# Grouped attention on one Trainium2 core: SP issues Q's loads between Q's stores and K's stores

## The reference, cut to what matters

```
q = (h @ Wq).reshape(b, s, H, HD)            # H = 16 heads, HD = 8
k = (h @ Wk).reshape(b, s, HKV, HD)          # HKV = 4 heads
v = (h @ Wv).reshape(b, s, HKV, HD)
q = _apply_rope(q, cos, sin)
k = _apply_rope(k, cos, sin)
...
scores = jnp.einsum('bqhd,bkhd->bhqk', q, k) / np.sqrt(HD).astype(np.float32)
scores = jnp.where(causal[None, None], scores, jnp.finfo(scores.dtype).min)
attn = jax.nn.softmax(scores, axis=-1)
ctx = jnp.einsum('bhqk,bkhd->bqhd', attn, v).reshape(b, s, H * HD)
```

## Time and profile before

| | us |
|---|---|
| median of 3 runs | 3165.83 |
| lowest, highest | 3156.24, 3166.15 |
| the profiled execution's own time | 3165.76 |
| its span, first to last instruction | 3164.0 |
| around the span (3165.76 - 3164.0) | 1.76 |
| grouped attention, about | 520 to 1260 |

### The profile page before, as it was taken

How to read it: one execution, slowest core, us unless ns; L and a number is a source line. 1 busy time by engine, 2 the same in 40 slices (tenths; PEclk the granted TensorE clock), 3 DMA queues, 4 the chain that set the end, 5 groups by cost and what they waited for, 6 DMA issues and landing times. The chain is left out here.

```text
span 3164.0 us, 66212 instructions
## 1 busy us (share of the span) xinstructions
PE 2882.8 (91%) x22258; PEld 1871.3 (59%) x22258; DVE 2482.6 (78%) x6944; ACT 2326.2 (74%) x3601; POOL 2104.2 (67%) x2402
## 2 busy tenths in 40 slices
PE   6999997788998888789579999999999999999979
PEld 3555554344444444678246666666666666666668
DVE  5777776788888875567468888888888888888867
ACT  5888883466666667444289999999999999999833
POOL 5666673346555543577657888788877888788745
PEclk8999997799999999899789999999999999999989
DMA  4544534223322330685400000000000000000001
GB/s 121 131 108 112 129 92 91 59 62 69 69 57 60 72 70 19 191 271 158 128 1 1 17 1 17 1 7 11 6 12 1 17 1 17 1 17 1 1 14 41
DMA packets 151509, 178.31 MB, mean 56 GB/s; under 512 B 18619, under 2 KB 122784, under 8 KB 151076
## 3 DMA queue, kind: packets, MB, share of 16 engines
q1 hardware_dynamic: 142084, 157.14, 19.2%
q0 software_dynamic: 9088, 16.94, 1.6%
HBM read 99.82 MB, written 75.95 MB: 56 GB/s over the span
## 5 line engine op out<-in xcount | busy, mean ns | idle before, releaser
L3380 PE MATMUL lb_FF<-lb_h,lb_w 128*128 128x512 f32 x1024 | 502.0, 592 | 0.0
L3609 DVE TENSOR_SCALAR lb_z<-lb_M,lb_mv,lb_rstd 128x128 f32<-128x128 f32 x1024 | 344.9, 398 | 3.3 <-POOL lb_rstd L3534 3.0
L3497 ACT ACTIVATE lb_h<-lb_H,lb_prm 128x512 f32<-128x512 f32 x512 | 327.5, 699 | 2.6 <-PE lb_H L3371 2.6
L3534 POOL TENSOR_TENSOR lb_rstd<-lb_rstd,half 128x4 f32<-128x4 f32 x256 | 260.8, 1019 | 37.2 <-issue 1.3
L3365 PE MATMUL lb_H<-lb_x1s,lb_w 128*128 128x512 f32 x512 | 273.0, 533 | 0.0
L3380 PEld LDWEIGHTS lb_FF<-lb_h,lb_w 128*128 128x128 f32 x1024 | 193.5, 189 | 89.9 <-issue 61.1
L3601 DVE BATCH_NORM_STATS2 lb_stats<-lb_M 128x6 f32<-128x128 f32 x1024 | 226.9, 284 | 15.5 <-PE lb_M L3324 9.0
L1649 POOL TENSOR_SCALAR_AFFINE_SELECT da_PT<-da_PT 128x1024 f32<-128x1024 f32 x128 | 149.1, 1165 | 133.4 <-ACT da_PT L1566 133.3
L3366 PE MATMUL lb_H<-lb_x1s,lb_w 128*128 128x512 f32 x512 | 203.3, 397 | 0.0
L3371 PE MATMUL lb_H<-lb_x1s,lb_w 128*128 128x512 f32 x512 | 202.7, 397 | 0.1
L3552 POOL CAST lb_x1s<-lb_x 128x512 fp32r<-128x512 f32 x128 | 78.3, 611 | 173.7 <-DVE lb_x L3634 173.7
(11 more groups left out here) (514 smaller groups left out, 8860.8 us busy)
## 6 DMA issues: line engine op xcount, KB each, us to landing
moe_w<-experts_dram SPq DMA_DIRECT2D x39, 384.0 KB, 3.2
da_qT<-da_stq SPq DMA_DIRECT2D x64, 192.0 KB, 4.1
da_kT<-da_stk SPq DMA_DIRECT2D x64, 192.0 KB, 3.8
moe_x<-moe_xs SPq DMA_DIRECT2D x39, 260.0 KB, 3.6
tc_g<-moe_ys SPq DMA_DIRECT2D x32, 256.0 KB, 3.5
ga_q<-ga_stq SPq DMA_DIRECT2D x20, 384.0 KB, 5.8
lb_split<-moe_parts SPq DMA_DIRECT2D x8, 896.0 KB, 6.4
da_stq<-da_parts SPq DMA_DIRECT2D x16, 384.0 KB, 2.4
```

Source lines behind the costliest of these rows:

```text
L3380: pe.matmul(FF[:, :], w2[:, k, :], h[:, k, :], start=(k == 0), stop=(k == KC - 1)).then_inc(ff_filled, 1)
L3497: act.activation(h[:, k, :], H[:, k % 2, :], ACT.Gelu_apprx_tanh, bias=col(FB1 + k, i)).then_inc(h_ready, 1)
L3534: pool.tensor_tensor(out[:, :], out[:, :], C["half"][:, 0:NT], ALU.pow).then_inc(done, 1)
L3609: last = v.tensor_scalar(z[:, t, :], M[:, t * P:(t + 1) * P], mv[:, t, 0:1], rstd[:, t:t + 1], ALU.subtract, ALU.mult)
```

## The change

SP issues `load_q(c2)` directly behind `store_q(c2)`, ahead of `store_k(c2)`. Before, both groups of stores came first. No instruction is added or removed, on no engine, and no semaphore count changes.

```
@@ -1065,8 +1065,8 @@
                 c, c2 = b + 1, b + 2
                 if exists(c2):
                     store_q(c2)
+                    load_q(c2)
                     store_k(c2)
-                    load_q(c2)
                     load_k(c2)
                 if exists(c):
                     store_max(c)
```

## The result

The changed kernel takes 3174.18 us (median of 7 runs, 3171.63 to 3180.1), the kernel before in the same comparison 3162.6 us (7 runs, 3156.24 to 3166.15). The ratio is 1.0043, with a 95% interval of 1.0031 to 1.0054: slower, by 11.6 us between the medians.

The account below looks back on a forecast made before the run. The prediction took PE's restart in each batch to be set by the landing of K's second load. It added 19 us of later landings and 7 us of lower clock to 3165.76, giving 3192 us, range 3170 to 3210.

Parts of the forecast that it names:

- The place and the mechanism: PE's restart once a batch follows K's second load, which the change delays by putting K's stores behind Q's loads.
- the chain after: From landing of Q's third store to landing of K's second load in the changed kernel: 12.4 us, against 11.0 before.
- SP's reactions: SP's delay after Q's third store lands and again after K's stores land, 0.05 us each.
- Q's loads, issue to second landing: From issue of Q's first load to landing of its second: 7.4 us, bounds 6.9 to 7.8.
- K's stores behind them: Time K's stores still need after Q's second load lands: 0.7 us, bounds 0.3 to 1.0.
- K's loads in an empty queue: K's two loads, issued only after K's stores land, from issue to last landing: 4.2 us, bounds 3.95 to 4.5.
- the 2 us absorbed: PE's later waits for DVE, in batches 11, 8 and a little in 5 and 13, hide about 2 us of 21.
- the clock: Longer PE stops send 5 further restarts to the lower clock level, 1.45 us each, 7 us.
- The late third stores: In batches 1, 4, 5, 12, 13 Q's loads now wait for Q's late third store: K lands 2.7 us later.
- Rival 1: K's stores are not held up by Q's loads, so K lands 1.5 us earlier: 3147 us, chance 0.08.
- Rival 2: The delay is absorbed by DVE after restarts, or the terms' cheap ends hold: 3170 us, chance 0.12.
- Rival 3: The terms' expensive ends, 13.4 us, with ten clock losses: 3216 us, chance 0.05 for beyond 3210.

Follow-up runs that it names:

- q_half: Kernel before, with K's stores issued between Q's two loads and K's loads last: 3150.8 us, ratio 0.9965 to the kernel before.
- the pair with the masks: after_mask8 against before_mask8, the mask repeated eight times in both: 0.9991 against 0.9963, slower by 0.28% or 9 us.
- wait_only: Kernel before, plus a wait of SP for the landing of Q's stores ahead of K's stores, loads not moved: ratio 1.0023 to the kernel before.
- before_again: The kernel before, unaltered, profiled a second time: 612.9 us from first to last of the 15 batches.
- after_again: The changed kernel, unaltered, profiled a second time: 3185.36 us in this single execution, 630.4 us from first to last batch.
- k_on_act: Changed kernel, with K's three stores issued by ACT on another queue instead of by SP: ratio 1.0007 to the kernel before.
- after_mask8: Changed kernel, with the mask of each batch's first max_scores done eight times, ahead of the waits for the loads: ratio 0.9991 to the kernel before.
- before_mask8: Kernel before, with the mask of each batch's first max_scores done eight times, ahead of the waits for the loads: ratio 0.9963 to the kernel before.
- q_half_fill: q_half, with the mask ahead of the waits, 20, 10, 10 and 5 times in batches 1 to 4, once in the others: 3143.3 us, ratio 0.9935.

## Why the prediction was right in kind and wrong in size

**The place and the mechanism: right.** In both kernels PE restarts 0.1 us behind the last landing in all but one or two batches, Q's loads are issued at once behind Q's third store, 2 us earlier, and K's stores land behind Q's second load, 0.58 us on the mean of 15 batches. K's start-up, hidden before, is exposed. q_half, which hides it again and keeps the rest, turned the loss into a gain.

**The step that failed is the sum for the chain after, 12.4 us.** The forecast was 1.4 us a batch over the 11.0 before; the two pairs of profiles have 0.77 and 0.80 (11.76 against 10.99, 11.98 against 11.18). By its own terms, means of the 15 batches in the two profiles of the changed kernel:

| term | forecast | first profile | second |
|---|---|---|---|
| SP's reactions | 0.10 | 0.03 | 0.03 |
| Q's loads, issue to second landing | 7.4 | 7.17 | 7.31 |
| K's stores behind them | 0.7 | 0.58 | 0.62 |
| K's loads in an empty queue | 4.2 | 3.97 | 4.02 |
| sum (of the unrounded terms) | 12.4 | 11.76 | 11.98 |

No term is far off, and each lies inside its bounds, but all err to the same side. The largest error beside Q's loads is K's loads, where the nearest row had the answer, 3.95 us, and I went above it. The quantity that counts is the difference to 11.0, so an error of 5% in the sum made 1.4 us a batch out of 0.77, 21 us out of 11.5. With the 2 us absorbed it is 19 forecast, where the batches show 11.3 and 13.0 and the pair with the masks 9 for this part. The second step that was mis-sized is the clock, 7 us forecast and 2.0 and 4.5 shown, both below.

**The late third stores: right in kind.** Batches 1, 4, 5, 12 and 13 lost 1.9, 1.9, 2.9, 1.9 and 2.3 us of the interval between Q's third store and the last landing, mean 2.2 where 2.7 was forecast. The other ten lost 0.06 us on the mean, where 0.75 was forecast. In the second pair of profiles it is 1.9 us for the five and 0.3 us for the ten. So most of the delay came from five batches: in the others Q's head start of 2 us nearly paid for K's exposed start-up. wait_only bears out that this wait alone costs something.

**What can hide the delay: nothing, on balance.** The intervals and the times for 15 batches in the table, without the kernels with masks repeated, lie on a line of 16.5 us per microsecond of interval, within 4 us; over the 14 steps from first to last that is 1.18 us of time for each microsecond of landing. More than one, probably because a longer stop also costs clock; the 2 us that DVE was to absorb do not show. The 14 steps can also be cut in two, at the last landing of each batch, which gives the landing's part and the rest directly (us in sum, two executions of each kernel):

| | before | before_again | changed | after_again |
|---|---|---|---|---|
| Q's first store to the last landing | 212.2 | 211.9 | 223.5 | 224.9 |
| from there to Q's next first store | 401.0 | 401.0 | 403.0 | 405.5 |
| both | 613.2 | 612.9 | 626.5 | 630.4 |

The landing is 11.3 and 13.0 us of the loss in these batches, and what comes behind PE's restart 2.0 and 4.5 us.

**The clock: the price right, the number too large.** The changed kernel's first profile has 11 restarts with a granted clock under 0.75, against 8, and the second pair 12 against 9. Three more, not five, at 1.45 us are 4 us where 7 were forecast. It was not that the longer stops stayed harmless: of the seven restarts that had been at the upper level, six went to the lower one (4, 5, 9, 11, 12, 13), but three others (6, 14, 15) came back up, which the forecast did not allow for. The price rested on one pair of restarts, and holds: in batch 9 the stretch from the last landing to Q's next first store takes 28.08 us in the kernel before, at a clock of 1.00, and 29.62 us in the changed one, at 0.71. Comparing the same batch over the 140 stretches of ten profiles (those without repeated masks and without ACT's stores) gives 1.4 us for the lower level.

**The rivals.** Rival 1 named the point that decides: K's stores landing before Q's second load. They land after it, so its gain was not to be had in this order; q_half reaches it another way. Rival 2 holds in neither form: DVE absorbed nothing that shows, and the sum was above its cheap ends, 11.25, though the measured delay of 0.8 us a batch lies between those, 0.25, and the forecast's 1.4. Rival 3's 13.4 was not reached in either profile's mean. The rule of the Trainium skill that was weighed there ("DMA: Bandwidth & Descriptors", "Rules for kernel authors": issue a DMA early, wait late) holds for Q's loads taken alone and was reversed by what they push back. Its neighbour in the same section of the Trainium skill says that spreading DMAs over the issuing engines' queues does not help bandwidth, since all run on the same 16 DMA engines and interleave. The trace of k_on_act agrees with the reason given: the 144 packets of K's own queue moved among those of Q's, and K's third store took 6.2 us. Bandwidth itself was not measured here. In the prediction and in the expectation for k_on_act I had put the order of landings down to the queue. The 400 pairs counted for it show less than they seem to: 238 of them share a semaphore, and for those the profile gives out the landings in the order of issue.

**The range** (3170 to 3210) holds the 3174.18 us; the point, 3192, is the part that was wrong.

## What to carry to other kernels

A transfer that is brought forward can put off what follows it on the DMA engines, so follow the chain of the one that lands last, not the one that moves; here it paid to issue a small store that others wait for ahead of a long load, and more to issue it between the load's halves. Where a forecast is the difference of two chains, the small difference carries the whole error: take the nearest row for each term as it stands, without rounding up, and give the difference its own range. A sum of several effects is better read by cutting the time where one ends and the next begins than from the difference of two edits, which brought an effect of their own here. A stop of PE that can't be removed can be filled with harmless matmuls, which here was worth 12 to 16 us, what they overran included.

## What the runs showed of the hardware that was not expected

- A store of 96, 64 and 32 KB in a queue of its own, issued by ACT while 768 KB of loads were under way, still landed only about when the loads had: in batch 2 6.2 us behind the issue of the third, and 0.0 to 0.9 us behind the last load in 12 of 15 batches, against 1.6 us into idle DMA engines. Their packets moved among those of the loads; the first started 1.5 to 4.2 us after the issue of the first store there, and 0.8 to 0.9 us after it in the three batches in which the stores went ahead.
- Q's third store lands late (up to 4.4 us after its issue in the kernel before and 4.8 in the changed one, instead of 2.7) in the same batches from one execution to the next (1, 4, 5, 12, mostly 13), and in others once PE's code is a little longer (1, 2, 6, 7, 8 in after_mask8 and before_mask8, 1, 6, 7, 14, 15 in q_half_fill). In batch 4 of the kernel before the profile has one instruction load among the packets, and behind it a trickle of packets of 12 to 23 GB/s, about one DMA engine's rate if 339 GB/s are 16 of them, 21 (DMA queues from 682.5 to 686 us; the digits are the busy tenths of 16 engines, then GB/s in 40 slices):

```profile
DMA  9999999995000000000000000000000000000098
GB/s 328 339 339 538 328 293 304 339 328 164 12 0 0 12 12 0 12 12 12 12 12 23 23 23 23 23 23 23 23 12 0 0 0 0 0 0 0 0 281 211
...
q8 instruction: 1, 0.02, 1.7%
```

The other profiles bear it out: in all 14, 210 batches, the third store took over 3.2 us in 70. In every one of these an instruction load of 16 KB (queue q8) started between 0.15 us before the store's issue and its landing. In none of the other 140 did one start between 0.15 us before the issue and 2.4 us after it, and those stores took at most 2.9 us. So an instruction load beside the store and a late landing go together, and since the late landings are where the changed kernel lost most, part of its loss hangs on where in the code these loads fall. That the load holds up one engine's share of the store fits this; no run took the loads away.

- A copy of 256 KB from memory to memory between two groups of loads put the last landing off by only 0.2 us.
